# Where a layer norm's last step stands, and on which engine, in a graph network of eight passes over one matrix

## The reference

```python
x = _layernorm(x + _L0_gnn_ref(...))   # adj @ (f * (adj @ (x @ W))), twice, relu between
x = _layernorm(x + _L1_gnn_ref(...))   # concat(x, adj @ x) @ weight
x = _layernorm(x + _L2_gnn_ref(...))   # (sigmoid(q @ k.T / scale + bias) * adj * adj) @ messages, then an update,
                                       # relu, a norm with gamma and beta
x = _layernorm(x + _L3_gnn_ref(...))   # silu((adj @ .) @ W + b), twice

def _layernorm(x, axis=-1, eps=1e-05):
    m = jnp.mean(x, axis=axis, keepdims=True)
    v = jnp.var(x, axis=axis, keepdims=True)
    return (x - m) / jnp.sqrt(v + eps)
```

## Time and profile before

| | |
|---|---|
| median of three runs | 1678.27 us (1678.04 to 1683.83) |
| the profiled execution | 1678.3 us |
| its span in the profile | 1676.0 us |
| mean granted TensorE clock | 0.992 |
| TensorE busy | 1613.0 us, 96% |
| VectorE busy | 1236.9 us, 74% |
| ScalarE busy | 1111.4 us, 66% |
| GpSimd busy | 59.5 us, 4% |
| DMA moved | 490.77 MB, mean 293 GB/s |

### The profile page before, as it was taken

One profiled execution on the slowest core, in us unless ns is written; L12 is line 12 of the kernel. 1 busy time (PEld: TensorE's weight loads), 2 busy tenths in 40 slices (PEclk: granted clock), 3 DMA queues, 4 the chain that ended last, 5 costly groups with the idle time before them and its releaser, 6 DMA issues. The chain is left out here.

```text
span 1676.0 us, 19175 instructions
## 1 busy us (share of the span) xinstructions
PE 1613.0 (96%) x7618; PEld 761.9 (45%) x7618; DVE 1236.9 (74%) x1185; ACT 1111.4 (66%) x789; POOL 59.5 (4%) x47
## 2 busy tenths in 40 slices
PE   7999999999999998999999899999998999999987
PEld 4444444444444444444554444344444444444433
DVE  5866537654766478657898698989999996455897
ACT  5667747764777577756666587787869676445753
POOL 2000000000000000000000000101000100000001
PEclk9999999999999999999999999999999999999999
DMA  9979798979799888996878255554545897665993
GB/s 355 419 301 381 288 409 353 372 284 395 300 389 427 341 314 348 373 351 267 324 285 319 101 203 186 180 187 176 214 163 210 323 391 280 251 233 187 349 343 143
DMA packets 68425, 490.77 MB, mean 293 GB/s; under 512 B 7824, under 2 KB 7984, under 8 KB 9328
## 3 DMA queue, kind: packets, MB, share of 16 engines
q1 hardware_dynamic: 67104, 485.00, 75.1%
q0 software_dynamic: 1088, 4.49, 0.8%
q10 hardware_dynamic: 144, 0.07, 0.0%
HBM read 420.32 MB, written 69.21 MB: 292 GB/s over the span
## 5 line engine op out<-in xcount | busy, mean ns | idle before, releaser
L921 DVE SCALAR_TENSOR_TENSOR a_lo<-a_ring,a_hi 128x2048 f16<-128x2048 f32 x332 | 750.8, 2289 | 291.2 <-ACT a_hi L742 287.0
L742 ACT ACTIVATE a_hi<-a_ring 128x2048 f16<-128x2048 f32 x332 | 627.6, 1905 | 284.8 <-PE spare L538 151.0
L538 PE MATMUL acc<-a_hi,y_hi 128*128 128x512 f16 x1584 | 475.6, 381 | 6.0 <-ACT a_hi L742 4.0
L538 PE MATMUL acc<-a_hi,y_lo 128*128 128x512 f16 x1584 | 474.7, 381 | 0.0
L550 PE MATMUL acc<-a_lo,y_hi 128*128 128x512 f16 x1584 | 418.4, 380 | 11.1 <-DVE a_lo L921 6.2
L550 PEld LDWEIGHTS acc<-a_lo,y_hi 128*128 128x128 f16 x1584 | 153.4, 98 | 203.3 <-DVE a_lo L921 12.0
L538 PEld LDWEIGHTS acc<-a_hi,y_hi 128*128 128x128 f16 x1584 | 155.1, 98 | 192.1 <-issue 12.0
L538 PEld LDWEIGHTS acc<-a_hi,y_lo 128*128 128x128 f16 x1584 | 155.5, 98 | 188.9 <-issue 3.4
L943 DVE SCALAR_TENSOR_TENSOR gates<-gates,a_ring 128x1024 f32<-128x1024 f32 x128 | 156.2, 1220 | 31.7 <-ACT gates L772 31.5
L755 ACT ACTIVATE a_hi<-gates 128x1024 f16<-128x1024 f32 x128 | 134.7, 1053 | 41.7 <-DVE gates L943 41.5
L930 DVE TENSOR_TENSOR a_lo<-gates,a_hi 128x1024 f16<-128x1024 f32 x128 | 155.9, 1218 | 0.0
(11 more groups left out here) (98 smaller groups left out, 691.6 us busy)
## 6 DMA issues: line engine op xcount, KB each, us to landing
a_ring<-adj_dram SPq DMA_DIRECT2D x332, 1024.0 KB, 7.4
saved_squares<-squares SPq DMA_DIRECT2D x64, 1024.0 KB, 12.6
a_ring<-saved_squares SPq DMA_DIRECT2D x64, 1024.0 KB, 4.8
x_T<-xt_dram SPq DMA_DIRECT2D x4, 512.0 KB, 8.8
x_rows<-x_dram POOLq DMA_DIRECT2D x1, 2048.0 KB, 13.0
out_dram<-x_rows POOLq DMA_DIRECT2D x3, 512.0 KB, 4.4
out_dram<-x_rows SPq DMA_DIRECT2D x2, 256.0 KB, 2.0
w<-W_dram POOLq DMA_DIRECT2D x2, 64.0 KB, 5.5
```

What stands on the lines that cost most here:

```text
L538: mm = pe.matmul(sums[:, h * BANK:(h + 1) * BANK], blk(y[:, y_pass % 2, :], st.j0 + s), slot(a_hi, st)[:, s, h * BANK:(h + 1) * BANK], sta ...
L742: act.activation(slot(a_hi, st), loaded(st), ACT.Copy, scale=2.0 ** A_EXP).then_inc(s_ahi, 1)
L921: dve.scalar_tensor_tensor(out=slot(a_lo, st).rearrange("p s c -> p (s c)"), in0=loaded(st).rearrange("p s c -> p (s c)"), scalar=2.0 ** A ...
```

## The change

In passes 4 and 5 `normalise` gets the position after that of `ln_moments`, where it stood in the same one; so one split of VectorE comes between them. In the last pass, for its chunks 0 to 2, `normalise` is replaced by `shift` on VectorE at the same position 6, and `normalise_again` on ScalarE at position 7. The counts of `s_shift`, the waits of `shift` and of GpSimd's `root` are put in general form to fit.

```diff
@@ PER_CHUNK
     "ln": {4: 1, 5: 1, 6: 1, 8: 1},
+    "shift": {6: 1, 8: 1},
@@ ScalarE
             def normalise_again(blocks):
                 def go(p, k):
-                    act.wait_ge(s_shift, k + 1)
+                    act.wait_ge(s_shift, nth("shift", p, k))
...
                 7: {0: [evacuate], 2: [sigmoid], 3: [y_high]},
-                8: {0: [evacuate], 2: [sigmoid]},
+                8: {0: [evacuate], 2: [sigmoid], 7: [normalise_again(range(CB))]},
@@ VectorE
             def shift(p, k):
 
-                dve.wait_ge(s_root, nth("root", p, k, 1))
+                dve.wait_ge(s_root, nth("root", p, k, PER_CHUNK["root"][p] - 1))
...
-                4: {0: [take_over], 1: [values, ln_moments(0, s_val, "val"), normalise], 5: [y_low]},
-                5: {0: [take_over], 1: [values], 2: [ln_moments(0, s_val, "val"), normalise],
+                4: {0: [take_over], 1: [values, ln_moments(0, s_val, "val")], 2: [normalise], 5: [y_low]},
+                5: {0: [take_over], 1: [values], 2: [ln_moments(0, s_val, "val")], 3: [normalise],
...
-                8: {0: [take_over], 2: [swish], 4: [residual], 5: [ln_moments(0, s_res, "resid")], 6: [normalise]},
+                8: {0: [take_over], 2: [swish], 4: [residual], 5: [ln_moments(0, s_res, "resid")], 6: [shift]},
@@ GpSimd
             def root(run):
                 def go(p, k):
-                    if p > GATED or (p == GATED and (run or k)):
-                        pool.wait_ge(s_ln, NC * (p - 4) + k if p == GATED else NC * 3)
+                    if p >= GATED:
+                        pool.wait_ge(s_ln, nth("ln", p, k) - 1)
...
             epilogue(stages, at, THE_END)
+            pool.wait_ge(s_ln, last("ln", 0))
             for h in range(HALVES):
```

## The result

The changed kernel takes 1681.82 us (median of 12 runs, 1678.9 to 1683.65) against 1677.87 before (12 runs, 1676.65 to 1683.83). The ratio is 1.0021, 95% interval 1.0013 to 1.0028: slower by 0.2%, as forecast (1681.8), and inside the 0.5% that the prediction calls no change. The interval lies above 1, so the loss itself is clear of the noise. The profiled execution has a span of 1679.7 us, 3.7 more than before.

What follows compares the result with a forecast made beforehand. TensorE, busy 96% of the span, was taken as the bound, so only its waits count; -1.8 +4.9 -1.8 -1.7 +2.9 +1.0 = +3.5 on 1678.3 gave 1681.8 us, range 1676 to 1687.

Steps and rivals of the forecast that it cites:

- no change: Whole kernel: a time within about 0.5%, 8.4 us, of the kernel before; chance 0.90.
- The power beside a split: Layer norms: GpSimd's power takes 3.55 us instead of 1.64 beside an `a_lo`, so VectorE gains only 0.2.
- Pass 5, chunks 0 to 2: Transposes of `x_rows` wait for the later normalisation, +1.64 us each, +4.9 in all.
- Pass 5, chunk 3: Chunk among gated units: the 2.25 us wait for L930 goes and the transposes start earlier, -1.8 us.
- the rule weighed there: Pass 5's fourth chunk: L930 would wait for the power on the shared SBUF port, total 1.2 us higher.
- Pass 8: Three chunks: ScalarE waits some 4.5 us for the shift with splits queued behind; 0.95 later each, +2.9 us.
- Pass 4: Four chunks, one `a_lo` moved ahead in each: -0.3, 0, -0.5 and -1.0 us, sum -1.8.
- The clock: TensorE's granted clock: the fall behind the 2.25 us wait goes, -1.7; 0.6 of a new fall, +1.0 us.
- the sum of +3.5: Whole kernel: -1.8 +4.9 -1.8 -1.7 +2.9 +1.0 us added to 1678.3, giving 1681.8.

Runs made afterwards that it cites:

- the PSUM experiment: Kernel before, with the VectorE split in pass 8's gap reading its second operand from PSUM instead of SBUF; the power beside it took 1.66 us, not 3.57.
- position 9: Kernel before with the edit of pass 8 alone, ScalarE's `normalise_again` at position 9 instead of 7; 1670.84 us, ratio 0.9953.
- position 9 with the fourth chunk: Kernel before with pass 8's edit, `normalise_again` at position 9, and the normalisation moved in pass 5's fourth chunk alone; 1670.55 us, ratio 0.9947.
- no wait for the power: Kernel before, but in passes 4 and 5 VectorE scales by a constant and doesn't wait for GpSimd's power; 1666.72 us, ratio 0.9931.

## Why the prediction was right

*The power beside a split.* Right in its numbers and, by the PSUM experiment, in its cause: 3.58 to 3.62 in the seven norms of passes 4 and 5 that have a split in the gap, 2.55 beside L944 and L931. The two lengths have one reading: the power ends 1.50 us after the VectorE instruction in whose time it began, at 812.97 after the split's end at 811.47, and at 947.51 after L944's end at 946.01.

*Pass 5, chunks 0 to 2.* Predicted +1.64 each, found +1.62 each. The experiment with these three alone has the same waits, and leaving them out of passes 4 and 5 gives 2.7 (by the ratios) to 3.9 (by the medians) back.

*Pass 5, chunk 3.* Predicted -1.8 and -1.7 for the clock; found -1.81 and -1.62. VectorE and the power, from the timeline of the changed kernel:

```profile
944.79 1.22 DVE L944 SCALAR_TENSOR_TENSOR gates<-gates,a_ring 128x1024 f32<-128x1024 f32 x1
945.93 1.22 DVE L931 TENSOR_TENSOR a_lo<-gates,a_hi 128x1024 f16<-128x1024 f32 x1
947.54 2.14 DVE L856 TENSOR_SCALAR x_rows<-val,moments,stats 128x128 f32<-128x128 f32 x8 [0.39 <-POOL stats L989]
...
944.96 2.55 POOL L989 TENSOR_TENSOR stats<-stats,neg_half 128x8 f32<-128x8 f32 x1 [56.33 <-DVE stats L843]
```

L931 runs in the middle of the power at its usual length. The total by the rule weighed there (Trainium skill, SBUF — State Buffer, "Who interferes with whom") was 1683.0 and by the rows 1681.8; here the rows held. The other half of that rule, GpSimd held by a VectorE instruction with two SBUF inputs and not by one with a single one, is what the PSUM experiment shows (1.66 against 3.57).

*Pass 8.* Predicted 0.95 three times; found +0.95, +0.97, and +0.24 together with the clock. ScalarE waits 4.66 where some 4.5 was forecast. The same instructions two positions later gain: it is ScalarE's queue.

*Pass 4.* Here a term was wrong. Chunk 0 gave -0.3, and the two waits of 0.47 in chunks 2 and 3 went, with -1.2, a little more than expected. But "VectorE comes there 0.2 earlier, and the `a_lo` that frees a ring slot stands 3.9 us earlier, so the loads start earlier; the gaps for `a_hi` on the way can go too: -1.0" failed: the step from 779 to 798 is +1.10, so for chunk 3 +0.5 instead of -1.0. (The gap ahead of 794.56 was also read as 0.58 where the earlier trace rows shows 0.48.) ScalarE's splits before and in the changed kernel, from the two timelines, before:

```profile
789.84 1.91 ACT L742 ACTIVATE a_hi<-a_ring 128x2048 f16<-128x2048 f32 x1 [1.37 <-DMA a_ring<-adj_dram]
792.61 1.91 ACT L742 ACTIVATE a_hi<-a_ring 128x2048 f16<-128x2048 f32 x1 [0.86 <-DMA a_ring<-adj_dram]
```

and after:

```profile
788.80 1.91 ACT L743 ACTIVATE a_hi<-a_ring 128x2048 f16<-128x2048 f32 x1 [1.93 <-DMA a_ring<-adj_dram]
792.70 1.91 ACT L743 ACTIVATE a_hi<-a_ring 128x2048 f16<-128x2048 f32 x1 [1.99 <-DMA a_ring<-adj_dram]
```

The last split ahead of `z_T` starts at 792.6 or 792.7, though VectorE was ready earlier: its load sets it. I had counted the gaps as going with an earlier issue. From 780 to 798 the DMA engines are busy 0.99 of the time in both kernels (398 and 387 GB/s), so a load asked for earlier mostly stands in line; that this is the limit is argued, not tested. In three more kernels in which TensorE was 0.7 to 2.2 us early at 779 (passes 4 and 5 alone, position 9, position 9 with the fourth chunk) it starts behind that `z_T` at 798.05 to 798.28. But with pass 5's three chunks alone it was 2.1 early and kept 1.9 of it, and with no wait for the power it started at 794.17. So the wall is not fixed in time, and what sets the loads' arrival I did not settle. Nor is the +1.10 shown to be the edit's: with pass 4 as before, this wait is 2.42 to 3.59 us in the traces of eight kernels, and with pass 4 edited 3.19 to 4.71 in four. What all four do show is that it never became shorter than before.

*The clock.* Predicted -1.7 and +1.0. In this execution it gave -3.3 (the falls at 926 and 947 missing), +0.8 and +1.4 at 650 and 798, and about -0.5 in pass 8, where one fall stands for another: near -1.6 where the forecast had -0.7. The waits of 1.46 ahead of the transposes, priced as possible new falls, were followed by none in any of the nine cases traced. So the sum of +3.5 is 0.2 off the 3.7 of the traces, with errors of opposite sign in it: +1.4 in pass 4, -0.9 in the clock, -0.3 from before pass 4, -0.2 in pass 8. That the time itself came out at 1681.82 is luck on top: the kernel before, taken as 1678.27 from three runs, has a median of 1677.87 over twelve, so the medians are 3.95 apart. The mechanisms carry the prediction, not its last digit.

## What to carry to other kernels

An instruction put into a wait hides it only if it leaves the awaited engine alone: look at a place where the two already run side by side before you move anything. And a step given to a less busy engine costs what is queued behind it there while it waits for its input; move it back by as many of that queue's items as the next consumer needs, which here turned a loss of 2.5 us into a gain of 7.9. What is moved later in time must be checked against its earliest reader: 0.4 us of slack against 2.0 of delay gave 1.6, three times.

## What was not expected of the hardware

Kernels that do the same at one place differ there by the clock's falls: TensorE's wait of 2.12 at 926 was followed by a granted clock of 0.50 for 3.4 us in the kernel before and by 1.00 in the changed one and in the kernel of pass 5's three chunks. Falls cost 1.7 us behind that wait of 2.12 and, behind waits of 3.54 and 3.56 for the same `z_T`, 3.0 in one kernel (granted clock 0.54 over 6.8 us) and 1.4 in another. The kernel before alone spread from 1675.6 to 1684.2 in 27 runs; whether the falls make that spread is not shown, since only one of its executions was traced. GpSimd's power of 128x8 elements goes from 1.64 to 3.6 us beside a VectorE instruction with two operands in SBUF and not at all (1.64 to 1.66, three times) beside one of equal size that reads one of them from PSUM.
